# A two-layer attention and mixture-of-experts kernel: queries, keys and maxima in three bfloat16 parts of 64 rows a head, and the causal mask added on TensorE

## Time and profile before

| What | us |
|---|---|
| median of three runs | 945.59 |
| the profiled execution, its own time | 943.85 |
| span of its profile | 942.1 |
| granted TensorE clock over the span | 0.897 of full |

### The profile page before, as it was taken

How to read it: one execution, slowest core, us unless ns; L and a number is a source line. 1 busy time by engine, 2 the same in 40 slices (tenths; PEclk the granted TensorE clock), 3 DMA queues, 4 the chain that set the end, 5 groups by cost and what they waited for, 6 DMA issues and landing times.

```text
span 942.1 us, 18341 instructions
## 1 busy us (share of the span) xinstructions
PE 834.8 (89%) x6319; PEld 501.3 (53%) x6319; DVE 720.9 (77%) x2077; ACT 546.7 (58%) x1202; POOL 282.3 (30%) x424
## 2 busy tenths in 40 slices
PE   7698999888879869999999999999987989898994
PEld 6354655455579733344344434344432434788994
DVE  5777788887265768898899888989895874786674
ACT  2355656546556524688788868687664765333431
POOL 6233334326412354204210011001025223344332
PEclk9799999998979966799999979799795988988997
DMA  5556523111103133244242403110251100102123
GB/s 156 189 169 195 179 80 108 41 47 36 43 21 96 56 102 125 72 160 145 112 151 69 136 25 105 47 58 25 83 177 51 47 7 21 42 27 78 42 64 113
DMA packets 68470, 82.43 MB, mean 87 GB/s; under 512 B 8295, under 2 KB 44391, under 8 KB 68057
## 3 DMA queue, kind: packets, MB, share of 16 engines
q1 hardware_dynamic: 40120, 46.11, 16.2%
q10 hardware_dynamic: 24960, 28.32, 9.6%
q0 software_dynamic: 3296, 6.82, 2.2%
HBM read 52.08 MB, written 37.80 MB: 95 GB/s over the span
## 4 chain that ended last, share of the span: by engine, by line
PE 55%; DVE 27%; issue 4%; DMA 4%; ACT 4%; POOL 3%; another core or an unknown queue 1%; SPq 1%; ACTq 1%; DVEq 0%; POOLq 0%
PE pv L1898 13%; PE st L1875 10%; DVE M L2199 9%; PE ring L2013 6%; PE ring L1866 5%; PE ring L1769 4%; DVE M L2206 4%; PE st L1998 4%; DVE ring L2203 3%; ACT Et L1623 2%; PE ring L1837 2%; PE st L2006 2%; PE st L1991 2%; PE pv L2006 2%; PE ring L1780 1%
## 5 line engine op out<-in xcount | busy, mean ns | idle before, releaser
L1623 ACT ACTIVATE Et<-st 128x512 f32<-128x512 f32 (+3 forms) x768 | 372.9, 545 | 149.8 <-PE st L1875 130.1
L2206 DVE TENSOR_REDUCE M<-ring 128x1 f32<-128x512 f32 x256 | 159.4, 683 | 29.8 <-PE ring L1866 23.6
L2199 DVE TENSOR_REDUCE M<-ring 128x2 f32<-128x512 f32 x256 | 159.9, 681 | 15.4 <-PE ring L1866 14.7
L1898 PE MATMUL pv<-Et,Va 128*32 128x256 f32 (+3 forms) x1536 | 146.5, 443 | 4.0 <-ACT PVs L1630 2.3
L2203 DVE CUSTOM_DVE_ANT_0 ring<-ring,maskw 128x128 f32<-128x128 f32 (+3 forms) x256 | 120.5, 512 | 36.0 <-PE ring L1866 33.5
L1875 PE MATMUL st<-Qs,Kbd 128*128 128x512 f32 (+3 forms) x256 | 90.0, 370 | 8.9 <-ACT Et L1623 7.5
L1898 PE MATMUL pv<-Et,RV 128*32 128x256 f32 x1024 | 92.4, 434 | 5.1 <-ACT PVs L1630 5.0
L1866 PE MATMUL ring<-Kbd,Qs 128*128 128x128 f32 (+3 forms) x256 | 84.6, 360 | 13.5 <-DVE M L2203 5.9
L1386 POOL TENSOR_SCALAR_AFFINE_SELECT Et<-Et 128x256 f32<-128x256 f32 x128 | 53.0, 419 | 128.0 <-ACT Et L1623 127.7
L1866 PE MATMUL ring<-RKT,Qs 32*128 32x512 f32 x256 | 84.4, 540 | 3.9 <-DVE M L2199 2.3
L1866 PE MATMUL ring<-KT,Qs 32*128 32x512 f32 x256 | 79.0, 553 | 8.9 <-DVE M L2206 8.3
(11 more groups left out here) (303 smaller groups left out, 1337.1 us busy)
## 6 DMA issues: line engine op xcount, KB each, us to landing
Qs<-Dq SPq DMA_DIRECT2D x46, 256.0 KB, 3.0
Xd<-Xd ACTq DMA_DIRECT2D x8, 1056.0 KB, 5.6
Dq<-hq SPq DMA_DIRECT2D x24, 256.0 KB, 3.2
Dk<-hk SPq DMA_DIRECT2D x16, 256.0 KB, 4.1
L1W<-in_L1W ACTq DMA_DIRECT2D x2, 2048.0 KB, 12.6
Kbd<-Dk SPq DMA_DIRECT2D x60, 64.0 KB, 2.0
KT<-Dk SPq DMA_DIRECT2D x15, 256.0 KB, 2.7
Dq<-Xq SPq DMA_DIRECT2D x12, 256.0 KB, 4.3
```

What stands on the lines that cost most here:

```text
L1623: e.activation(Et[s // 2 % 4][:, j % 2, q0:512], bank(ph)[:, q0:512], ACT.Exp, scale=SCALE).then_inc(exp_done, 1)
L1898: ins = nc.tensor.matmul(pv[32 * j:32 * j + 32, cols], v, Et[s // 2 % 4][:, j % 2, cols], start=first and (l == 0 or what == "pva"), stop= ...
L2199: e.tensor_reduce(M[i][:, t, j, :], bank(ph)[:, :].rearrange("p (two n) -> p two n", two=2), AX.X, ALU.max).then_inc(mx_red, 1)
L2206: e.tensor_reduce(M[i][:, t, j, 0:1], bank(ph)[:, 0:n], AX.X, ALU.max).then_inc(mx_red, 1)
```

## The change

- A head has 64 rows (`HR`) in bfloat16: eight rows for each of 8 numbers, six of them products of three parts (`NPART`), one spare (`MAXROW`) for the maxima. Four heads need 256 rows: `Qs`, `KT` and `RKT` become [128 rows, 2, 512], head j in rows 64*(j%2) on, slot j//2. `Kbd`, its zero fills, and `k0put` go; layer 0 uses `KT` too, with four buffers, one DMA a unit.
- `mx` and `st` use 64 rows in both layers. In layer 0 `mx` is followed by a second matmul, a bfloat16 identity times the diagonal block of the mask, into the last 128 columns of the bank; VectorE takes a plain maximum there too.
- `split` casts to bfloat16, GpSimd subtracts (`low`), VectorE casts again (`mid`), GpSimd subtracts again (`last`). For the first batch of each layer all eight operations are VectorE's. The first unit is now made from these parts by `sel`: 12 matmuls of 512 columns with a 0/1 matrix `pick`, taken by ScalarE (keys) and VectorE (queries). `k0`, `q0`, `k1`, `q1` and `u` go.
- Staging: still six DMAs, each writing its part one to three times over, 1.5 MB a batch as before, in 1 KB pieces instead of 2 KB. `mput`: three DMAs a unit instead of two, six for "rec" instead of four.
- Maxima are cut in three by truncation: `mcol` is two subtractions in place of a masking and a subtraction. The past keys are cut and turned in the same way (`pastkv`, `pastK`).
- Some steps move: the projections of layer 0 begin 4 steps earlier, two of layer 1 by 2.

```diff
...
-        for piece in range(6 if keys else 3):
-            if piece < (4 if keys else 2):
-                do("low", l, b, k, piece)
-            do("stage", l, b, k, piece)
+        if k == 0:
+            for piece in (0, 3, 1, 4, 2, 5):
+                do("stage", l, b, k, piece)
+                yield
+            return
+        for side in range(1 + keys):
+            do("low", l, b, k, 2 * side)
+            do("low", l, b, k, 2 * side + 1)
+            do("stage", l, b, k, 3 * side)
             yield
+        if keys:
+            yield
+        do("mid", l, b, k)
+        yield
+        for side in range(1 + keys):
+            do("last", l, b, k, 2 * side)
+            do("last", l, b, k, 2 * side + 1)
+            do("stage", l, b, k, 3 * side + 1)
+            yield
+        for side in range(1 + keys):
...
-            yield
         for what in ("pq", "pk", "split"):
             do(what, 1, 0, 0)
+            yield
+        for s in range(2):
+            do("sel", 1, "k", s)
+            do("sel", 1, "q", s)
             yield
         do("vp", 1, 0, 0)
...
+                        e.dma_start(of[:, 0:3, :], Pq[0][:, :].unsqueeze(1).broadcast_to([128, 3, 512])).then_inc(q_staged, 16)
+                    elif piece == 1:
+                        sp.wait_ge(q_mid, n + 1)
+                        e.dma_start(of[:, 3:5, :], Pq[1][:, :].unsqueeze(1).broadcast_to([128, 2, 512])).then_inc(q_staged, 16)
...
-                            e.dma_start(Kbd[u % 3][32 * j:32 * j + 32, j, :].bitcast(F32), Dk[slot][4 * g + j, :, :]
-                                        ).then_inc(kbd_in[u % 3], 16)
-                    else:
+                    if l:
                         sp.wait_ge(*keys_let_go(u))
-                        e.dma_start(KT[u % NK][:, :].bitcast(F32), Dk[slot][4 * g:4 * g + 4, :, :].rearrange("j r n -> (j r) n")
-                                    ).then_inc(kt_in[u % NK], 16)
+                    elif u >= NK:
+                        sp.wait_ge(st_full, n_st["st", 0, u - NK, 3, 3] + 1)
...
                 elif what == "mput":
                     l, u = a
-                    wide = 4 if units[l][u][0] == "rec" else 2
+                    many = 2 if units[l][u][0] == "rec" else 1
                     q = Qs[q_no(l, u) % NQ]
                     sp.wait_ge(*taken(("mT", l, u)))
-                    for m in range(wide):
-                        e.dma_start(q[24 + m:128:32, :].bitcast(F32), Ms[l][u % 2][16 * m:16 * m + 16, :]).then_inc(m_in[u % 2], 16)
+                    for m in range(NPART * many):
+                        m16 = 32 // many * m
...
+                        e.tensor_tensor(Xk[:, sl], Xk[:, sl], Pk[0][:, sl], ALU.subtract).then_inc(k_low, 1)
+                elif what == "last":
+                    l, b, k, piece = a
+                    n0 = 256 * (piece % 2)
+                    sl = slice(n0, n0 + 256)
+                    if piece < 2:
+                        pool.wait_ge(q_mid, n_split["split", l, b, k] + 1)
...
+                elif what == "sel":
+                    l, of, s = a
+                    pe.wait_ge(ld["pick"], 16)
+                    if of == "k":
+                        pe.wait_ge(k_last, 2 * n_ksplit["split", l, 0, 0] + 2)
+                    else:
+                        pe.wait_ge(q_last, 2 * n_split["split", l, 0, 0] + 2)
+                    parts, n0 = (Pq, 0) if of == "q" else (Pk, 6)
+                    for i in range(NPART):
+                        ins = nc.tensor.matmul(bank(ph)[:, :], pick[:, n0 + 3 * s + i, :], parts[i][0:32, :], start=(i == 0),
+                                               stop=(i == NPART - 1))
+                    ins.then_inc(misc_full, 1)
                 elif what in ("pq", "pk"):
                     l, b, k = a
...
+                    ins = nc.tensor.matmul(bank(ph)[:, 0:n], Qs[q_no(l, u) % NQ][r, s, t * 128:(t + 1) * 128], keys[:, 0:n],
+                                           start=True, stop=(l == 1), skip_group_check=True)
+                    if l == 0:
+                        pe.wait_ge(ld["id"], 16)
+                        pe.wait_ge(ld["mask"], 16)
+                        ins = nc.tensor.matmul(bank(ph)[:, n - 128:n], tops(ident[:, :]), tops(maskw[:, 384:512]), start=False, stop=True,
+                                               skip_group_check=True)
+                    ins.then_inc(mx_full, 1)
                 elif what == "st":
                     l, u, c, j = a
                     kind, k, b, g = units[l][u]
                     q0 = 128 * c if l == 0 else 0
-                    r = slice(32 * j, 32 * j + 32) if l else slice(0, 128)
-                    keys = RKT[r, g, :] if kind == "rec" else KT[u % NK][r, :] if l else Kbd[u % 3][:, j, :]
+                    r, s = rows_of(j), j // 2
+                    keys = RKT[r, g, s, :] if kind == "rec" else KT[u % NK][r, s, :]
                     pe.wait_ge(*m_ready(l, u))
-                    nc.tensor.matmul(bank(ph)[:, q0:512], keys[:, c * 128:(c + 1) * 128], Qs[q_no(l, u) % NQ][r, q0:512],
+                    nc.tensor.matmul(bank(ph)[:, q0:512], keys[:, c * 128:(c + 1) * 128], Qs[q_no(l, u) % NQ][r, s, q0:512],
                                      start=True, stop=True).then_inc(st_full, 1)
                 elif what in ("pva", "pv"):
                     l, u, c = a
...
                     dve.wait_ge(*taken(("pq", l, b, k) if has_keys(l, k) else ("rq", b, k)))
                     if n:
...
-                    high(hq[:, :], Xq[:, :]).then_inc(q_high, 1)
-                    if has_keys(l, k):
-                        n = n_ksplit[ph]
...
-                        if n:
-                            dve.wait_ge(k_staged, 48 * n)
-                        high(hk[:, :], Xk[:, :]).then_inc(k_high, 1)
+                        if nk:
+                            dve.wait_ge(k_staged, 48 * nk)
+                        e.tensor_copy(Pk[0][:, :], Xk[:, :]).then_inc(k_high, 1)
+                    if k == 0:
+                        dve.wait_ge(q_high, n + 1)
+                        e.tensor_tensor(Xq[:, :], Xq[:, :], Pq[0][:, :], ALU.subtract).then_inc(q_low, 2)
+                        dve.wait_ge(k_high, nk + 1)
+                        e.tensor_tensor(Xk[:, :], Xk[:, :], Pk[0][:, :], ALU.subtract).then_inc(k_low, 2)
+                        dve.wait_ge(q_low, 2 * n + 2)
+                        e.tensor_copy(Pq[1][:, :], Xq[:, :]).then_inc(q_mid, 1)
+                        dve.wait_ge(k_low, 2 * nk + 2)
+                        e.tensor_copy(Pk[1][:, :], Xk[:, :]).then_inc(k_mid, 1)
+                        dve.wait_ge(k_mid, nk + 1)
+                        e.tensor_tensor(Pk[2][:, :], Xk[:, :], Pk[1][:, :], ALU.subtract).then_inc(k_last, 2)
+                        dve.wait_ge(q_mid, n + 1)
...
-                        e.tensor_reduce(M[i][:, t, j, :], bank(ph)[:, :].rearrange("p (two n) -> p two n", two=2), AX.X,
+                        e.tensor_reduce(M[:, 3 * i, c:32:16], bank(ph)[:, :].rearrange("p (two n) -> p two n", two=2), AX.X,
                                         ALU.max).then_inc(mx_red, 1)
-                    elif l == 0:
-                        dve.wait_ge(ld["mask"], 16)
-                        e.tensor_tensor_reduce(bank(ph)[:, 0:n], bank(ph)[:, 0:n], maskw[:, 512 - n:512], 1.0, -3e38,
-                                               ALU.add, ALU.max, M[i][:, t, j, 0:1]).then_inc(mx_red, 1)
-                    else:
-                        e.tensor_reduce(M[i][:, t, j, 0:1], bank(ph)[:, 0:n], AX.X, ALU.max).then_inc(mx_red, 1)
+                    else:
+                        e.tensor_reduce(M[:, 3 * i, c:c + 1], bank(ph)[:, 0:n], AX.X, ALU.max).then_inc(mx_red, 1)
...
-                    elif l == 1:
-                        dve.wait_ge(y_full, before(("between",), "output"))
-                    else:
-                        dve.wait_ge(z_mc, 1)
+                    wide = 32 if kind == "rec" else 16
+                    m0, m1, m2 = (M[:, n, 0:wide] for n in (3 * (u % 2), 1, 2))
+                    had = earlier(ph, ("mT",), lambda p: True)
+                    if had is not None:
+                        dve.wait_ge(misc_full, filled(had))
                     dve.wait_ge(mx_red, last_max(l, u))
-                    halves(hi, lo, M[u % 2][:, :, :, :] if kind == "rec" else M[u % 2][:, :, :, 0]).then_inc(mcol_done, 1)
+                    step(e.tensor_tensor(m1, m0, tops(m0), ALU.subtract))
...
```

360 lines of the change are left out of this document (162 added, 198 removed).

## The result

The changed kernel takes 1019.03 us (median of four runs, 1012.34 to 1029.96), the kernel before beside it 945.4 us; the ratio is 1.073, with a 95% interval of 1.066 to 1.080. (The ratio leaves out the run of 1029.96 us, which lies over 1.5% above the fastest, and so is a little under the quotient of the medians, 1.078.) The forecast was 957 us with a range of 922 to 988; the time is 62 us above it, in the direction that the sum already had. The profiled execution took 1020.85 us with a span of 1019.1, against 943.85 and 942.1 before.

The account below looks back on a forecast made before the run. No engine full: attention 0 bound by a loop through the maxima's landing, attention 1 by VectorE, or TensorE at half clock. +3.5 - 4 + 4 + 8 = +11.5 gave 955.4, forecast 957 us, range 922 to 988.

Parts of the forecast that it names:

- Attention 0, -4 (-10 to +8): Layer 0's attention: third DMA, plain maxima, TensorE's steps with the mask matmul, and earlier keys together change it by -4 us.
- The third DMA, +8: Attention 0: the third `mput` transfer lies fully on the loop, 15 x 0.53 us, +8 us.
- Plain maxima, -5: Attention 0: VectorE's plain maxima save about 0.05 us for each of seven, 15 x 0.35 us, -5 us.
- The fourth key buffer, -3: Attention 0: with the one key DMA it frees units from late keys, -3 us (0 to -5).
- Opening, +3.5 (2 to 6): Before the first `mx`: projections, casts, subtractions and `sel` add 4.5 us; unit 1's keys in one DMA give back 1.
- End of experts 0, +4 (1 to 6): Before layer 1: TensorE waits 3.0 us for the cast chain, and `sel` takes 2.8 us where `u` took 1.7; +4 us.
- Attention 1, +8: Layer 1's attention: +10 for TensorE's pairs, +4 for VectorE's casts, +1 for DMAs, -7 for the clock; +8 us.
- TensorE's +10: Attention 1: a pair goes from 1.06 to 1.15 us, partly covered by VectorE's 1.20; +10 us (2 to 35).
- strips of 64 rows don't stream side by side: Rival, attention 1: a pair takes 1.65 us, +115 us over VectorE's pace, about 1060 us in all; chance 0.04.
- TensorE becomes the bound: Slower rival, attention 1: a pair passes VectorE's 1.20 us, so projections and gates are added; 986 us, chance 0.28.
- The clock holds: Faster rival: denser matmuls lift half clock in attention 1 and weight loads are short; 931 or 923 us, chance 0.25.
- rival E: Raised with the experiments, attention 0: two matmuls side by side in different halves bring the low clock, not the rows; no chance given.

Follow-up runs that it names:

- e10_same_half: The changed kernel with layer 0's `mx` going through the heads as 1, 0, 3, 2, against the kernel before: 985.83 us, ratio 1.068.
- e9_zero_vec: Changed kernel with layer 0's keys zero-padded to 128 rows and its mask given back to VectorE, against the kernel before: 931.21 us, ratio 1.011.
- e7_zero_rows: Changed kernel with layer 0's keys zero-padded so `mx` and `st` read 128 rows, mask still on TensorE, against the kernel before: 951.33 us, ratio 1.005.
- e12_best: Changed kernel with layer 0 zero-padded to 128 rows, only zero halves cleared, opening's fillers and memset moved, `sel` four steps later, against the kernel before: 926.12 us, ratio 1.003.
- e1_mask_alone: Kernel before with only layer 0's mask moved to TensorE and a plain maximum on VectorE, against the kernel before: 928.97 us, ratio 1.0066.
- e6_open_late: Changed kernel with the Va1 memset held back, fillers moved before `sel`, layer 1's `sel` two steps later, against the kernel before: 1019.47 us, ratio 1.074.

## Why the prediction was wrong

*Attention 0, -4 (-10 to +8); measured +57.* The step that failed is TensorE's: "Side by side they take the longer's 0.23, and the mask's matmul adds between 0.06 ... and 0.25 ... I take 0.33, near the low end, because the loads in rows 4 hide behind the stream." Two things in it were wrong, the overlap and the mask's cost. The overlap: the section on the change and the prediction alike put the `st` and the `mx` behind it in different halves of the rows. For the first seven `st` of a unit, the very ones that the estimate was for, they are in the same half and follow each other 0.22 us apart; the order of heads in the code would have told. The mask: the 0.25 was the right end, and for another reason, two changes of rows and not a load. Together the step is 0.64, beyond the bound of 0.48 and against 0.41 before; by an estimate from these numbers, the 105 steps cost 24 us more even at full clock, where the sum gave back 4. With the long ones in different halves (`e10_same_half`) the step is 0.49, still beyond the bound. The price of a change of rows was not in the trace of before for layer 0: there `st` and `mx` both had 128 rows. The second failed step is the premise of the sum, the clock of 1.00 in the earlier trace rows, kept at 1.00 without a word on why 64 rows should keep it. It had seen half clock begin after gaps in TensorE's stream; in the changed kernel it also began at 32.7 and at 292.1 us, with no gap over 0.05 us in its stream since 21.1 and 283.3 us. The text named "a clock share in attention 0 well under 1.00, which no term here prices" as what would make it wrong; it was 0.75. Of these two steps the runs show the sizes together, in the 57 us, and only in part each by itself. No rival held them: all three looked for TensorE's bound and the clock's change in attention 1.

The other terms of that stage were small, and off too. The third DMA, +8: at most 2 to 4 at full clock, 7.5 in the stage as changed. Plain maxima, -5: nothing, or up to 3 us the other way (`e9_zero_vec` against `e7_zero_rows` and `e12_best`), where the mask's matmul and the plain maximum come together; that VectorE did not lead over those seven maxima is the likely reason, not a shown one. The fourth key buffer, -3, was not tried by itself.

*Opening, +3.5 (2 to 6); measured +9.1.* The chain on VectorE ran as foretold: from 16.96 to 21.51 us, the 4.5 us of the sum. What failed: "then a copy out and the start of the array, 1 us" after the last `sel`. In the trace:

```profile
21.06 0.80 PE L1843 MATMUL ring<-Pk,pick 32*128 32x512 bf16 x3 [3.91 <-DVE Pk L2191]
21.70 0.81 PE L1843 MATMUL ring<-Pq,pick 32*128 32x512 bf16 x3
22.35 1.33 PE L1843 MATMUL ring<-Pk,pick 32*128 32x512 bf16 x3
23.48 1.48 PE L1843 MATMUL ring<-Pq,pick 32*128 32x512 bf16 x3
24.89 2.08 PE L1861 MATMUL ring<-wqkv,hT 128*128 128x128 f32 x8
26.76 1.92 PE L1822 MATMUL pv<-onesM 128*128 128x128 f32 x8
28.61 0.28 PE L1881 MATMUL ring<-KT,Qs 64*128 64x128 bf16 x1
```

Value projection and fillers (L1861, L1822) stand between `sel` and the first `mx`: 3.7 us. They stood there before as well, but beside the copies that `mx` waited for even after them (0.68 us). After 3.9 us without work the clock falls within `sel` (0.80 becomes 1.3 to 1.5). And 1.5 us come from the memset above. Before, it stood behind the zero fills of `Kbd`, the first of which waited for `xh`; with `Kbd` that wait went, which the sum had at nothing. The fillers moved and the memset held back gave 3 to 5 of the 9 us.

*End of experts 0, +4 (1 to 6); measured +9.4.* The wait of 3.0 us was 3.9. The rest is the clock again; from the chain:

```profile
391.69 0.70 DVE Pk L2191
392.40 0.14 issue
392.53 2.71 PE ring L1843 x6
395.24 2.00 PE ring L2034 x8
397.25 2.67 PE ring L1843 x6
399.92 2.00 PE st L2012 x8
```

Twelve `sel` take 5.4 us instead of 2.8, and the groups of expert matmuls between them 2.00 us instead of 0.89. The stall was priced, the half clock that began in it (391 to 405 us) was not. With `sel` four steps later (`e12_best`) TensorE waits 0.36 us ahead of the first one and 0.64 ahead of the last three, and the stretch is 1.8 us over before.

*Attention 1, +8; measured about 0 (-0.6, and -2.8 ahead of it).* Here the prices of a pair held; the clock's term was too small. A pair in the chain of the changed kernel, at full clock:

```profile
501.71 0.32 PE st L1896 x2
502.03 0.22 PE ring L1881 x2
502.24 0.57 PE pv L1919 x8
```

and at half clock:

```profile
442.64 0.54 PE st L1896 x2
443.18 0.43 PE ring L1881 x2
443.61 1.01 PE pv L1919 x8
```

1.11 us where 1.15 was foretold and 1.06 stood before; 1.98 at half clock where 2.1 was foretold (1.73 before). VectorE's 1.20 covers the one, not the other. Half clock went from 107 to 52 us, more than the -7 that I gave it: by the prediction's own -17 for all 107 us, 55 us less are worth an estimated 9, and that is about what TensorE's +10 cost. VectorE was busy 91.73 of the 100 us from 520 to 620, all at full clock, where 88% was foretold and 92% stood before. On the quicker chip both forms of layer 1 took the same as well: 418.6 us with the f32r form (`e1_mask_alone`, 77 at half clock), 416.6 to 420.4 with the changed one (33 to 40). The load of bfloat16 weights, bounds 0.05 to 0.20, taken at 0.10, stands in the groups by line and form (busy us, mean ns):

```profile
L1896 PEld LDWEIGHTS st<-Qs,KT 64*128 64x128 bf16 x512 | 38.7, 95 | 115.9 <-issue 63.2
```

95 ns against 201 in the earlier trace rows. The Trainium skill (TensorE: Matmul & The Clock Gate, Weight-path perf modes) has the 32 cycles of the prediction's estimate as the theory, and for fp8; its measured row for trn2 says about 2x, and that is what this trace shows.

*The rivals.* That strips of 64 rows don't stream side by side is refuted (starts together at 144.57). "TensorE becomes the bound" came true, in attention 0 and not in attention 1: VectorE still leads in the latter, where its maxima are a third of the chain from 476 to 780 us, the largest part, and it is busy 339 of 389 us. "The clock holds" came true in attention 1 and failed in attention 0, by the same edit: layer 1 went from strips of 32 rows to 64, layer 0 from 128 to 64. That this is why is argued, not shown: no run changed the rows of layer 1 alone.

*What stays open.* In attention 0 the kernels whose score matmuls address more rows had the higher granted clock; the runs don't show by what rule it is granted, nor do they part the rows from rival E to the end. In the changed kernel and `e6_open_late` the same code had 124 to 158 us of half clock in attention 0, so no run here foretells it closely. How the 61 us between 205 (mask on VectorE, 128 rows) and the changed kernel's 266 divide can be said only in part: some 15 by row changes, some 11 by 64 rows alone, and some 35 by the two together. That these are the slack's doing, TensorE having none left, fits its 96% of busy time but is argued.

## What to carry to other kernels

Before narrowing a matmul to fewer rows, list what stands beside it on TensorE, and read from the code's order which half of the rows each neighbour is in: two matmuls in one half don't overlap, and each change between row counts costs 0.10 us here, more than a matmul of 128 columns. Zeros in the other rows were not waste here, as row count and granted clock stayed up with them: price an edit that narrows the matmuls at half clock too, and ask whether the engine then still has slack. Two edits that each use up the same engine's slack are to be priced together, since the sum of their single costs (3 and 11 us) said nothing of both (60) here.
